# Second attention: three tiles of probabilities added up on VectorE in four pieces, the others on GpSimd

## What is computed

```
def attend_1(q_x, kv_x, ...):                  # 16 heads of 32, 4096 queries, 3202 keys
    q, k, v = heads of layernorm(q_x) @ Wq.T and layernorm(kv_x) @ Wkv.T
    attn = jnp.einsum('bhqd,bhkd->bhqk', q, k) * scale
    attn = jax.nn.softmax(attn, axis=-1)
    out = jnp.einsum('bhqk,bhkd->bhqd', attn, v)
    x = q_x + out @ Wo.T + bo
    return x + silu(x @ W1.T + b1) @ W2.T + b2
```

## Time and profile before

| | us |
|---|---|
| median of 3 runs | 5864.05 |
| lowest, highest | 5859.81, 5869.54 |
| profiled execution | 5857.08 |
| its span | 5855.3 |

### The profile page before, as it was taken

One profiled execution on the slowest core, in us unless ns is written; L12 is line 12 of the kernel. 1 busy time (PEld: TensorE's weight loads), 2 busy tenths in 40 slices (PEclk: granted clock), 3 DMA queues, 4 the chain that ended last, 5 costly groups with the idle time before them and its releaser, 6 DMA issues. The chain is left out here.

```text
span 5855.3 us, 104136 instructions
## 1 busy us (share of the span) xinstructions
PE 5452.1 (93%) x28932; PEld 3433.4 (59%) x28932; DVE 3789.4 (65%) x6648; ACT 3159.7 (54%) x5849; POOL 2632.7 (45%) x1284
## 2 busy tenths in 40 slices
PE   5959999999969979999999999999999998699999
PEld 4834444444437746666565665656656664577777
DVE  4448888888846667777777777777767776332231
ACT  3327777777743336666666666666666665222222
POOL 0000000000000049999999999999989999000000
PEclk9969999999979979999999999999999999899999
DMA  3451111111134331111111111111111110422230
GB/s 100 124 128 27 35 34 36 34 34 35 30 96 123 105 98 39 30 39 39 40 39 41 28 40 40 39 41 38 30 38 41 40 27 20 135 87 83 74 96 22
DMA packets 328587, 325.58 MB, mean 56 GB/s; under 512 B 184624, under 2 KB 192688, under 8 KB 326064
## 3 DMA queue, kind: packets, MB, share of 16 engines
q1 hardware_dynamic: 328112, 319.92, 20.6%
HBM read 219.18 MB, written 100.53 MB: 55 GB/s over the span
## 5 line engine op out<-in xcount | busy, mean ns | idle before, releaser
L762 DVE TENSOR_REDUCE a_maxes<-a_mscore 128x1 f32<-128x458 f32 (+4 forms) x5632 | 3048.7, 604 | 981.8 <-PE a_mscore L807 971.5
L745 ACT ACTIVATE a_prob<-a_score 128x512 f32<-128x512 f32 x4992 | 2602.0, 606 | 1403.3 <-PE a_score L816 1401.7
L816 PE MATMUL a_score<-a_q,a_k 97*128 97x512 f32 (+1 forms) x4992 | 2035.8, 446 | 84.7 <-ACT a_prob L745 63.4
L807 PE MATMUL a_mscore<-a_k,a_qm 96*128 96x458 f32 (+4 forms) x5632 | 1971.3, 410 | 54.5 <-DMA a_k<-k 53.6
L715 POOL TENSOR_TENSOR a_added<-a_added,a_prob 128x1024 f32<-128x1024 f32 x768 | 1837.2, 2392 | 90.6 <-ACT a_prob L745 34.1
L835 PE MATMUL a_acc<-a_prob,a_v 128*32 128x512 f32 x9984 | 1646.4, 622 | 0.2 <-ACT a_prob L745 0.2
L807 PEld LDWEIGHTS a_mscore<-a_k,a_qm 96*128 96x128 f32 (+1 forms) x5632 | 1554.2, 310 | 120.0 <-issue 55.0
L816 PEld LDWEIGHTS a_score<-a_q,a_k 97*128 97x128 f32 (+1 forms) x4992 | 914.5, 194 | 1189.4 <-ACT a_prob L745 632.7
L712 POOL TENSOR_TENSOR a_added<-a_prob 128x1024 f32<-128x1024 f32 x128 | 305.4, 2386 | 2222.0 <-ACT a_prob L745 2221.5
L830 PE MATMUL a_acc<-a_prob,a_ones 128*1 128x512 f32 x2048 | 970.3, 596 | 0.0
L835 PEld LDWEIGHTS a_acc<-a_prob,a_v 128*32 128x32 f32 x9984 | 295.6, 110 | 251.3 <-issue 198.6
(11 more groups left out here) (187 smaller groups left out, 3791.2 us busy)
## 6 DMA issues: line engine op xcount, KB each, us to landing
a_qm<-q SPq DMA_DIRECT2D x384, 64.0 KB, 1.8
a_q<-q SPq DMA_DIRECT2D x384, 64.0 KB, 1.8
acc<-a_acc_sb SPq DMA_DIRECT2D x384, 64.0 KB
e_part<-acc SPq DMA_DIRECT2D x90, 256.0 KB, 3.5
a_k<-k SPq DMA_DIRECT2D x48, 416.0 KB, 5.9
q<-m_qout SPq DMA_DIRECT2D x128, 128.0 KB, 2.3
e_wo<-wo_split SPq DMA_DIRECT2D x32, 512.0 KB, 4.3
k<-kv_out SPq DMA_DIRECT2D x30, 512.0 KB, 2.7
```

The lines of the kernel that those rows point to most:

```text
L745: act.activation(prob[:, t], score[SCORES[it.j][t]][:], ACT.Exp, scale=SCALE).then_inc(exp_done, 1)
L762: dve.tensor_reduce(maxes[j][:, t, c:c + 1], mscore[u % UNIT_BANKS][:, 0:wide], AX.X, ALU.max).then_inc(unit_read, 1)
L807: pe.matmul(mscore[u % UNIT_BANKS][:, 0:wide], qm[j][r:r + ROW, t:NB:NB // P], kt[kk][r:r + ROW, at:at + wide], start=True, stop=True).the ...
L816: pe.matmul(score[SCORES[it.j][t]][:], kt[it.k][r:r + C, i * P:(i + 1) * P], qt[it.j][r:r + C, :], start=True, stop=True).then_inc(score_d ...
```

## The change

Tiles 22, 23 and 24 are added up by VectorE (`add_up`): four reduces of 128 queries x 3 tiles each, whose inner step goes from tile to tile (512 elements), into `vsum`. The four pieces of an item stand on VectorE behind the maxima of tiles 0 to 3 of the next item; those of the last item stand behind its last maxima. GpSimd leaves out the add of tiles 22 and 23 and that of 24, and adds `vsum` to `total` at the end: nine adds. ScalarE's exponential 22 waits for the pieces of the item before, and its waits for GpSimd are cut to the adds that read `prob` (`READ_BY`). The weighings move from tiles 3, 7, 11, 17, 23 to 3, 9, 14, 19, 25, ScalarE's copy from ahead of exponential 8 to ahead of 10, and the six units that are not one per tile are laid out anew.

```
-            self.at = {3: (3, True), 7: (4, True), 11: (0, False), 17: (1, False), 23: (2, False)}
-            self.copy_at = 4
+            self.at = {3: (3, True), 9: (4, True), 14: (0, False), 19: (1, False), 25: (2, False)}
+            self.copy_at = 5
-            more = {3: 2, 18: 2}
+            more = dict(enumerate([2, 1, 1, 0, 1, 2, 1, 1, 1, 0, 1, 2, 1, 1, 1, 1, 1, 2, 1, 1, 1, 1, 2, 1, 1, 0]))
...
-ADDS = 10
+ADDS = 9
+ON_VECTOR, PIECES = range(22, 25), 4
+READ_BY = 7
...
+            vsum = sb("vsum", [P, NB], F32)
...
@@ gpsimd
-                for i in range(1, 8):
+                for i in range(1, 7):
...
-                pool.wait_ge(add_done, base + 7)
-                pool.tensor_tensor(added[:, 0], added[:, 0], prob[:, 24], ALU.add).then_inc(add_done, 1)
+                pool.wait_ge(add_done, base + 6)
                 pool.tensor_tensor(added[0:LAST_KEYS, 1], added[0:LAST_KEYS, 1], prob[0:LAST_KEYS, 25],
                                    ALU.add).then_inc(add_done, 1)
-                pool.wait_ge(add_done, base + 9)
+                pool.wait_ge(add_done, base + 7)
...
                 pool.tensor_tensor(total[:], added[:, 0], added[:, 1], ALU.add).then_inc(add_done, 1)
+                pool.wait_ge(add_done, base + 8)
+                pool.wait_ge(vsum_done, it.n * PIECES + PIECES)
+                pool.tensor_tensor(total[:], total[:], vsum[:], ALU.add).then_inc(add_done, 1)
@@ scalar
-                        last = max(L.batches[b][-1], 1)
-                        act.wait_ge(add_done, it.n * ADDS - ADDS + (last if b < NBATCH - 1 else ADDS))
+                        last = min(max(L.batches[b][-1], 1), READ_BY - 1)
+                        act.wait_ge(add_done, it.n * ADDS - ADDS + (last if b < NBATCH - 1 else READ_BY))
+                if APART and t == ON_VECTOR[0] and not it.first:
+                    act.wait_ge(vsum_done, it.n * PIECES)
@@ vector
+            def add_up(n, i):
+                if i == 0:
+                    dve.wait_ge(exp_done, n * ST + ON_VECTOR[-1] + 1)
+                    dve.wait_ge(add_done, n * ADDS)
+                cols = slice(i * NB // PIECES, (i + 1) * NB // PIECES)
+                dve.tensor_reduce(vsum[:, cols], prob[:, ON_VECTOR[0]:ON_VECTOR[-1] + 1, cols].rearrange("p t c -> p c t"),
+                                  AX.X, ALU.add).then_inc(vsum_done, 1)
...
+                    if APART and t < PIECES and not it.first:
+                        add_up(it.n - 1, t)
+                if APART and it.last:
+                    for i in range(PIECES):
+                        add_up(it.n, i)
```

More of the change, by code:

```diff
@@ L561, in attention @@
         unit_done, unit_read, neg_done = sem("unit_done"), sem("unit_read"), sem("neg_done")
-        add_done, acc_copied = sem("add_done"), sem("acc_copied")
+        add_done, acc_copied, vsum_done = sem("add_done"), sem("acc_copied"), sem("vsum_done")
         acc_stored = [sem(f"acc_stored{i}") for i in range(2)]
```

## The result

| | before | after |
|---|---|---|
| median of 5 runs, us | 5863.15 | 5828.78 |
| lowest, highest | 5859.81, 5869.54 | 5819.64, 5839.98 |
| profiled execution (span) | 5857.08 (5855.3) | 5819.64 (5817.8) |

The ratio is 0.994, with a 95% interval of 0.9926 to 0.9955: the change takes 34 us off, where 63 were forecast.

A forecast was written before the change was run, and what follows sets the result against it. TensorE, busy 499 of 500 us in the second attention, was taken as the bound. From 5864 us, 57 for the weighings' places and 6 for the stage's end gave 5801; range 5780 to 5972 (8 in 10).

The forecast's parts named there:

- the prediction's own signs: Second attention: pieces under 0.56 us right, over 0.7 wrong; item 21.5 to 21.6 us right, 22 or more wrong.
- The weighings' new places: Second attention: moved weighings remove waits of scores for exponentials; 0.45 us per item, 57 us at 126 items.
- The strided pieces: VectorE's four reduces per item: each holds VectorE for d = 0.485 us, taking strided reads at the usual pace.
- the rival of slow strided reads: VectorE's pieces pay a stride penalty, d about 0.85, adding 161 us: 5962 us, slower; chance 0.26.
- The deadline at tile 7: Unit at 5.75 needs an earlier maximum finished: d under 0.53, beyond which TensorE stops 4 x (d - 0.53) per item.
- the walk: Timeline of an item from score 0: VectorE's maxima and pieces end at 2.99 + 4d, checked against two deadlines.
- GpSimd off the path: GpSimd's adds: 2.4 us less work per item, giving nothing in steady items because nobody waited for GpSimd.
- The end of the stage: VectorE's weight split moves behind the last item's sums: 11.5 us go, the later end costs some back; net -6 us.
- The one without a gain: Second attention: ScalarE's pace ends the waits at other tiles as often; only the stage end moves, 5858 us; chance 0.06.
- the blocking: VectorE's pieces and GpSimd's adds block each other, stalling TensorE 2.4 us per item: 6103 us; chance 0.04.
- Half of it: VectorE's pieces: d between 0.60 and 0.70, costing 0.48 us per item, 60 back: 5861 us, no change; chance 0.14.

## Why the prediction was right, and where it was wrong

The direction held, and so did the mechanism of the gain, the new places; the size was 63 and came out as 34. By the prediction's own signs it is a near miss: a piece takes 585 ns (under 560 was right, over 700 wrong), an item 21.66 us (21.5 to 21.6 was right, 22 wrong).

- **The weighings' new places, 0.45 us an item.** Right: 22.00 to 21.51 where they stand alone, 0.49, or 61 us. Score 0 no longer waits for its exponential, and loads of scores wait 100 instead of 142 us in all.
- **The strided pieces, d = 0.485.** Right, 0.51 from start to start, 585 ns alone for 550. The reason for doubt was a real one: a penalty of 0.7 ns an element, where 0.95 was read off TensorE's loads, comes with columns apart, and then the time is 5962.87; the rival of slow strided reads had 5962. That this fits to 1 us is luck: d is 0.77 there and not 0.85, and the deadline is 0.47 and not 0.53. That three tiles with adjacent columns escape the penalty no row of before could tell; on this term 0.485 was a choice that came out well.
- **The deadline at tile 7, d under 0.53.** The step that failed. It was counted to the start of the matmul of the unit (5.75), but what waits for the maximum is the weight load ahead of it, which starts at 5.54 where nothing holds it, and the pieces end 0.09 later than the walk had them. The margin of 0.2 us was none: 0.15 us an item were lost, 19 us in all. The threshold is 0.47.
- **GpSimd off the path.** Right: it waits 2.96 us per item (351.8 / 119) and nobody for it. Its relief of 2.4 us an item brings nothing; with all ten adds and the new places the time is no worse.
- **The term that wasn't there.** The sum took all 126 items to be alike. At the starts of heads the row of maxima stands behind the K and V loads. It came 0.4 us later and was due 0.4 us sooner, and score 0 waited for it. The prediction named the store and the row on SP's queue ("which is due only at tile 16"), but for the items within a head alone, and did not walk the queue where K and V are loaded. These waits were some 13 us by the run with the row first. The five turns of the loop, which the sum left out too, are in both kernels (some 23 us in before and 19 in after).
- **The end of the stage, -6.** Measured -12.7 in front and +5.3 behind, -7.4. From the last exponential to the load it is 19.5 us where 17.8 were forecast: the split took 16.9 beside GpSimd's last adds and not 15.5, and the load came 1.1 behind it and not 0.4.
- 57 less 43 (the median items), and 15 for what these leave out, make 29; a better end of the stage gives 1.4 back. That is the distance from 63 to 34 within 2 us.
- **The other rivals.** The one without a gain fell (an item went down 0.34), and so did the blocking: casts and two-operand work of VectorE slowed GpSimd at the end, the reduces did not (L729 runs beside the first piece and takes 1.29 us as it does before, L784 585 ns). "Half of it" was true in kind, TensorE stopping for the pieces, at a third of its size: 19 us where it had 60.

## What to carry to other kernels

Work that goes onto an engine with idle time must be walked against the deadline of the next buffer it frees, and that deadline is the weight load, not the matmul. When two edits come together, time each alone: here one carried all of the gain and the other took about a third of it back. After an edit in a steady loop, walk the queue of SP once at each place where the loop isn't steady (a new head, a turn, the end), since a small transfer behind large ones costs there what it never costs inside; and before moving work to the end of a phase, look for what the barrier waits for.

## What the runs showed of the hardware

- VectorE's reduce over a strided inner dimension is nearly free with three rows and adjacent columns (585 ns for 384 elements, some 550 by the adjacent pace), and costs 0.7 ns an element more with the columns four apart (858), or with four or five rows (1051 for 512, 1268 for 640, against 809 for 640 adjacent ones).
- Weight loads of TensorE held back by some 0.1 us each show in no list of waits, and still an item was 0.15 us longer.
- With four and five tiles a piece TensorE waited up to 2.0 and 2.5 us for a maximum, and its granted clock was 0.95 and 0.88 from 2300 to 4900 us, 1.00 with the columns apart; by estimate this cost up to 1.2 and 3.3 us an item on top of the wait.
- A turn of the loop over pairs holds TensorE for 2.6 us and mostly leaves it at 1.2 GHz for a while behind (0.84 granted over 11 us, at the last turn 1.00); the five turns and what follows them cost 20 us.
- The first load of the next phase came 1.1 us behind the end of VectorE's split wherever that ended last (three kernels).
